# A three-layer graph network kernel: the normalised rows are split to fp16 before they are transposed, and the DMA queue transposes them

## The chip, the cores and the metric

The kernel runs on one core of one Trainium2 chip. The metric is the time of one launch on the device, in microseconds (us). The engines are PE (matrix products), ACT (activations and copies), DVE (element-wise work and statistics), POOL (element-wise work, SBUF only) and SP, which only issues DMAs. Each runs its own list of instructions in order, and they meet through semaphores.

## The reference

The input is 128 graphs of 128 nodes with 256 features, in float32, and an adjacency matrix for each. The rows are normalised and clipped at zero, then three layers of attention over neighbours and a feed-forward block of width 1024 follow, and the input is added at the end.

```python
h = jnp.maximum(_layernorm(x), 0.0)
for l in range(3):
    si, sj = x @ attn_w[l, :d], x @ attn_w[l, d:]
    scores = si[:, :, None] + sj[:, None, :] + attn_b[l]
    scores = where(scores >= 0, scores, 0.2 * scores); scores = where(mask, scores, -inf)
    agg = einsum('bij,bjd->bid', softmax(scores), x)
    h = layernorm(x + agg, g1[l], beta1[l])
    ff = gelu(h @ W1[l] + b1[l]) @ W2[l] + b2[l]
    x = layernorm(h + ff, g2[l], beta2[l])
```

## The kernel before

Four graphs (T = 4) are one group, and one layer of one group is an item: 32 groups by 3 layers make 96 items. The items go in rings of RING = 4 groups: four groups in layer 0, the same four in layer 1, then in layer 2. All five engines run the same list of slots (L119); a slot has 8 steps, c = 0 to 7, one for each block of 128 hidden features (L440, L540, L714). The program is written out in full; there are no loops on the chip.

Every float32 product is made of three fp16 products: hi by hi, lo by hi, hi by lo, where hi is the value rounded to fp16 and lo is the rest.

Slot s works on several items at once. In step c the feed-forward block of item s makes hidden block c: PE (L357, 6 matmuls), ACT a Gelu in place and a rounding to g_hi (L477), DVE the rest g_lo (L569). PE then uses block c - 3 for the second product (`feed`, L373, 12 matmuls). PE may be three hidden blocks ahead of g_lo (PF_RING), so the first hidden product of the next slot waits for g_lo of step 5.

Between these stands the attention of item s + 2: dot products of its rows with two vectors (`dot_products`, L606, DVE, step 1), their spread over columns by PE transposes (L398, step 4), scores, row maxima and `minus_max` (L625, L635, DVE, step 4), exponentials (L507, ACT, after step 5; they need another activation table, loaded before them and another one after), PE transposes of the probabilities (`transpose_probs`, L410, step 7). In step 0 of the next slot, where it is item s + 1, PE makes the sums over neighbours (`aggregate`, L416). DVE adds them to the rows and takes statistics (L649 and L660, at the end of its step 7, though PE's part stands in the next slot's step 0; L582 aggregates them in step 0), POOL makes the inverse deviation (L786), and ACT writes the normalised rows norm1 (`norm_attention`, L500, after step 2).

Norm1 of item s + 1 is then turned: PE transposes it in float32 in 8 pieces (`transpose_norm1`, L429, step 4) into the PSUM banks that the second product of item s + 1 will use; ACT rounds the result to hT_hi (`high_hT`, L530, step 4); DVE makes hT_lo from PSUM (`split_hT`, L669, step 5). hT_hi and hT_lo have two buffers each. The first hidden product of the next slot waits for hT_hi, its fifth matmul for hT_lo.

POOL goes through its slot in this order (L838): inverse deviation, `h_residual` (L793, two passes over 1024 elements, from norm1), `low_X` (L805, one pass, writes X_lo), then for item s - 1 the inverse deviation, `norm_feed` (L809) and `layer_output` (L818, four passes of 512). In layer 2 the output goes to y_out, and `skip_connection` (L831) adds the input.

Each slot whose item s + 4 is in layer 0 also loads, normalises and masks a new group (DVE steps 5 and 6, ACT step 7): 32 of the 96. SP issues the loads and the stores, in an order of its own (L330 to L351). The PSUM is full: three banks of hidden blocks, one for scores and probabilities, and four in two pairs.

Of the kernel before, what the change touches and what calls it, by code (L numbers as in the profile page):

```python
# [41 lines left out]
RING = 4  # L42
# [55 lines left out]

def is_item(r, s):
    return not isinstance(r, int) or 0 <= PER * r + s < ITEMS  # L100
# [29 lines left out]
def gnn_kernel(nc, x, adj, attn_w, attn_b, W1, b1, W2, b2, g1, beta1, g2, beta2, out):  # L130
    with ExitStack() as ctx:
# [12 lines left out]
        minus_half = sb("minus_half", [P, T])  # L144
        w1_f32 = sb("w1_f32", [P, KD, H])
# [21 lines left out]
        x_again = [sb(f"x_again{i}", [P, T, D]) for i in range(2)]  # L167
        y_out = [sb(f"y_out{i}", [P, T, D]) for i in range(2)]
# [19 lines left out]
        hT_hi = [sb(f"hT_hi{i}", [P, KD, TN], F16) for i in range(2)]  # L188
        hT_lo = [sb(f"hT_lo{i}", [P, KD, TN], F16) for i in range(2)]
# [23 lines left out]

        def nT_banks(s):
            return p_pair[s % 2][:].rearrange("p (k u) d -> p k (u d)", k=KD)
# [33 lines left out]
        nT_psum = sem("nT_psum")  # L249
# [25 lines left out]
        def _(sp):  # L275
            def weights(l):
                if l >= 1:
                    sp.wait_ge(w_lo_ready, 4 * l - 2)
                    sp.wait_ge(bias_psum, l)
                sp.dma_start(w1_f32[:], W1[l].rearrange("(k p) h -> p k h", p=P)).then_inc(w_dma[0], 16)  # L280
                if l >= 1:
                    sp.wait_ge(w_lo_ready, 4 * l)
                sp.dma_start(w2_f32[:], W2[l].rearrange("(c p) d -> p c d", p=P)).then_inc(w_dma[1], 16)

            def graphs(tensor, g):

                v = tensor.rearrange("(g t) n d -> n g t d", t=T)
                if isinstance(g, int):
                    return v[:, g]
                return v[:, bass.ds(g, 1)].rearrange("n g t d -> n (g t) d")  # L290

            def load_x(g, i):
                sp.dma_start(x_in[i][:], graphs(x, g)).then_inc(x_loaded[i], 16)

            def load_adj(g, i):
                sp.dma_start(adj_in[i][:], graphs(adj, g)).then_inc(adj_loaded[i], 16)

            def load_again(g, i):
                sp.dma_start(x_again[i][:], graphs(x, g)).then_inc(x_again_loaded[i], 16)

            def store(g, i):
                sp.dma_start(graphs(out, g), y_out[i][:]).then_inc(stored[i], 16)

            load_x(0, 0)
            load_adj(0, 0)
# [7 lines left out]
            load_x(1, 1)  # L313
            load_adj(1, 1)
            weights(0)
            for g in (2, 3, 4, 5):
                sp.wait_ge(x0_ready, 4 * (g - 1))
                load_x(g, g % 2)
                sp.wait_ge(mask_steps, 2 * (g - 1))
                load_adj(g, g % 2)  # L320
                if g == 2:
                    for dst, v in ((g1_rows, g1), (b2_rows, b2), (res_rows, beta1), (g2_rows, g2), (beta2_rows, beta2)):
                        sp.dma_start(dst[:].rearrange("p l d -> p (l d)"),
                                     flat(v).partition_broadcast(P)).then_inc(rows_dma, 16)
                if g in (3, 4):
                    weights(g - RING + 2)
            load_again(0, 0)
            load_again(1, 1)

            for r in range(LOOPS - 1):  # L330
                for q in range(RING):
                    i, g = q % 2, r * RING + q

# [8 lines left out]
            for g in range(RING * (LOOPS - 1), G):  # L342
# [7 lines left out]
                if g + 2 < G:  # L350
                    load_again(g + 2, g % 2)  # L351
# [421 lines left out]
        def _(pool):  # L773
# [64 lines left out]
            def slot(r, s):  # L838
# [6 lines left out]
                if is_item(r, s + 2):  # L845
                    low_X(r, s + 2)
# [32 lines left out]
```

## Time and profile before

| | before |
|---|---|
| median of 3 runs | 2461.77 us (2460.39 to 2462.76) |
| profiled execution, own time | 2464.22 us |
| its span | 2462.4 us |
| PE, DVE, ACT, POOL busy | 95%, 85%, 77%, 69% |
| granted TensorE clock, mean | 0.993 |

PE stands near its limit over the whole span, and DVE not far below. A share of busy time does not say what sets the length of a slot, so a slot has to be followed in the order of time. In the rows below, times are microseconds from the start of the span, and the first two numbers of a row are start and length. A row with "x4" holds four instructions that follow one another, and its length is that of all four. Instructions that overlap in an engine's pipe show lengths that are greater than the distance of their starts.

### The profile page before, as it was taken

How to read it: one execution, taken by the hardware profiler on the slowest of the kernel's cores; microseconds unless marked ns; L12 is line 12 of the kernel's file. 1: busy time of each engine (PE TensorE's matmuls, PEld its weight loads, DVE VectorE, ACT ScalarE, POOL GpSimd, SP SyncE). 2: the span in 40 equal slices, each digit the busy share in tenths (PEclk: the TensorE clock that was granted, in tenths of full speed). 3: DMA queues.
4: the chain of work that ended last, by engine and by line, in shares of the span. 5: the costliest groups of instructions: out<-in, count | busy, mean ns of one | idle time of the engine just before them, and what ended most of it. 6: DMA issues, size and time to landing. Idle time of an engine off the chain costs nothing.

```text
span 2462.4 us, 47718 instructions
## 1 busy us (share of the span) xinstructions
PE 2350.7 (95%) x16608; PEld 1648.4 (67%) x16608; DVE 2097.8 (85%) x6070; ACT 1890.0 (77%) x3402; POOL 1701.0 (69%) x1540
## 2 busy tenths in 40 slices
PE   3999999999999999999999999999999999999997
PEld 2766666676666666667666666666666666666765
DVE  6778998888988899888988889988898889988884
ACT  4767788877787878787787777877778777878783
POOL 3457677767776767766786667776678676777675
PEclk9999999999999999999999999999999999999998
DMA  5200012000210002100021001200012000110001
GB/s 170 73 1 1 1 44 78 1 1 1 74 48 1 1 14 61 48 1 1 14 78 31 1 1 31 73 18 2 1 44 61 18 2 1 44 52 1 1 1 52
DMA packets 77422, 70.84 MB, mean 29 GB/s; under 512 B 7040, under 2 KB 75648, under 8 KB 77184
## 3 DMA queue, kind: packets, MB, share of 16 engines
q1 hardware_dynamic: 77184, 67.79, 9.1%
q8 instruction: 134, 2.20, 0.4%
q14 instruction: 104, 0.85, 0.1%
HBM read 51.01 MB, written 16.78 MB: 28 GB/s over the span
## 4 chain that ended last, share of the span: by engine, by line
DVE 55%; PE 19%; ACT 13%; issue 10%; POOL 0%; DVEq 0%; POOLq 0%
DVE g_lo L573 11%; DVE bn L580 9%; PE p_pair L383 8%; DVE res L656 6%; DVE dots L614 6%; ACT probs L514 5%; PE p_hid L369 5%; ACT L514 5%; DVE res L681 5%; DVE scores L632 4%; DVE dots L617 4%; PE p_pair L425 3%; DVE row_top L638 3%; DVE minus_max L642 2%; PE p_att L413 2%
## 5 line engine op out<-in xcount | busy, mean ns | idle before, releaser
L383 PE MATMUL p_pair<-w_hi,g_hi 128*128 128x256 f16 x3072 | 839.1, 273 | 0.0
L383 PE MATMUL p_pair<-w_lo,g_hi 128*128 128x256 f16 x3072 | 838.8, 273 | 0.0
L383 PE MATMUL p_pair<-w_hi,g_lo 128*128 128x256 f16 x3072 | 838.8, 273 | 0.0
L481 ACT ACTIVATE p_hid<-p_hid,b_eff 128x512 f32<-128x512 f32 x768 | 504.5, 657 | 328.6 <-PE p_hid L369 327.4
L573 DVE TENSOR_TENSOR g_lo<-p_hid,g_hi 128x512 f16<-128x512 f32 x768 | 527.5, 687 | 239.4 <-ACT g_hi L486 232.9
L801 POOL TENSOR_TENSOR h_res<-norm,g_rows 128x1024 f32<-128x1024 f32 x96 | 227.7, 2372 | 395.8 <-DVE res L681 389.1
L486 ACT ACTIVATE g_hi<-p_hid 128x512 f16<-128x512 f32 x768 | 458.5, 597 | 24.3
L369 PE MATMUL p_hid<-hT_hi,w_hi 128*128 128x512 f16 x1536 | 458.7, 380 | 2.3 <-DVE g_lo L573 2.3
L369 PE MATMUL p_hid<-hT_hi,w_lo 128*128 128x512 f16 x1536 | 458.9, 380 | 0.0
L369 PE MATMUL p_hid<-hT_lo,w_hi 128*128 128x512 f16 x1536 | 458.8, 380 | 0.0
L789 POOL TENSOR_TENSOR rstd<-var_eps,minus_half 128x4 f32<-128x4 f32 x224 | 241.6, 1079 | 307.4 <-DVE minus_mean L588 302.1
L383 PEld LDWEIGHTS p_pair<-w_lo,g_hi 128*128 128x128 f16 x3072 | 301.2, 98 | 107.3 <-issue 0.8
L383 PEld LDWEIGHTS p_pair<-w_hi,g_hi 128*128 128x128 f16 x3072 | 301.2, 98 | 106.2 <-issue 1.0
L383 PEld LDWEIGHTS p_pair<-w_hi,g_lo 128*128 128x128 f16 x3072 | 301.2, 98 | 35.5
L491 ACT ACTIVATE norm<-res,shift,rstd 128x256 f32<-128x256 f32 x384 | 199.3, 589 | 102.0 <-POOL shift L791 102.0
L369 PEld LDWEIGHTS p_hid<-hT_lo,w_hi 128*128 128x128 f16 x1536 | 150.8, 98 | 182.6 <-issue 2.5
L369 PEld LDWEIGHTS p_hid<-hT_hi,w_lo 128*128 128x128 f16 x1536 | 150.7, 98 | 182.5 <-issue 2.2
L580 DVE BATCH_NORM_STATS2 bn<-res 128x6 f32<-128x256 f32 x768 | 268.9, 414 | 3.3
L803 POOL TENSOR_TENSOR h_res<-h_res,res_rows 128x1024 f32<-128x1024 f32 x96 | 226.9, 2363 | 7.5
L587 DVE TENSOR_SCALAR var_eps<-mv 128x4 f32<-128x4 f32 x224 | 213.4, 953 | 7.7
L815 POOL TENSOR_SCALAR norm<-res,rstd,shift 128x256 f32<-128x256 f32 x384 | 209.8, 561 | 10.0
L656 DVE SCALAR_TENSOR_TENSOR res<-p_pair,row_inv,X 128x256 f32<-128x256 f32 x384 | 159.0, 477 | 65.5 <-PE p_pair L425 65.5
(67 smaller groups left out, 3855.2 us busy)
## 6 DMA issues: line engine op xcount, KB each, us to landing
x_in<-in_x SPq DMA_DIRECT2D x32, 512.0 KB, 5.3
x_again<-in_x SPq DMA_DIRECT2D x32, 512.0 KB, 5.1
out<-y_out SPq DMA_DIRECT2D x32, 512.0 KB, 3.3
adj_in<-in_adj SPq DMA_DIRECT2D x32, 256.0 KB, 5.6
w_f<-in_L_gnn_W SPq DMA_DIRECT2D x6, 1024.0 KB, 5.6
attn_rows<-in_L_gnn_attn_w SPq DMA_DIRECT2D x1, 768.0 KB, 5.6
g_rows<-in_L_gnn_g SPq DMA_DIRECT2D x2, 384.0 KB, 8.3
b_rows<-in_L_gnn_b SPq DMA_DIRECT2D x1, 384.0 KB, 7.4
```

What stands on the lines that cost most here:

```text
L369: mm = pe.matmul(p_hid[in_ring(s, c, PF_RING)][:], w[l][:, k, cols], h[i][:, k, :], start=(n == 0), stop=(n == 3 * KD - 1))
L383: mm = pe.matmul(ff_banks(s)[:, t, :], g[i][:, nodes], w[l][:, c, :], start=(c == 0 and t % 2 == 0 and n == 0), stop=(c == C - 1 and n == ...
L481: act.activation(p_hid[k][:], p_hid[k][:], ACT.Gelu, bias=b1_eff[:, l, c:c + 1], scale=1.0 / WSCALE).then_inc(gelu_ready, 1)
L486: act.activation(g_hi[i][:], p_hid[k][:], ACT.Copy).then_inc(g_hi_ready, 1)
L514: act.activation(probs[:, t, :], leaky[:, t, :], ACT.Exp, bias=minus_max[:, t:t + 1], accum_out=row_sum[:, t:t + 1]).then_inc(probs_ready, 1)
L573: dve.tensor_tensor(g_lo[i][:], p_hid[k][:], g_hi[i][:], ALU.subtract).then_inc(g_lo_ready, 1)
L580: dve.bn_stats(bn[n][:, t, :], src[:, t, :]).then_inc(stat_steps[n], 1)
L587: dve.tensor_scalar(var_eps[n][:], mv[n][:, :, 1], EPS, None, ALU.add).then_inc(stat_steps[n], 1)
L656: dve.scalar_tensor_tensor(out=res1[:, t, :], in0=agg_banks(s)[:, t, :], scalar=row_inv[:, t:t + 1], in1=X[s % RING][:, t, :], op0=ALU.mul ...
L789: pool.tensor_tensor(rstd[n][s % 2][:], var_eps[n][:], minus_half[:], ALU.pow).then_inc(rstd_ready[n], 1)
L801: pool.tensor_tensor(h_res[i][:], norm1[:], rows(g1_rows, l, T), ALU.mult).then_inc(h_res_steps, 1)
L803: pool.tensor_tensor(h_res[i][:], h_res[i][:], rows(res_rows, l, T), ALU.add).then_inc(h_res_steps, 1)
```

## The change

- The 8 float32 transposes of norm1 on PE are gone. ACT rounds norm1 to h_hi in SBUF (`high_h`) in step 3, ahead of `high_X`, where `high_hT` stood in step 4. DVE makes h_lo = norm1 - h_hi, both inputs in SBUF (`low_h`), in step 4, ahead of the scores, where `split_hT` stood in step 5. SP issues two DMA transposes of 128x1024 fp16 for each item (`turn_h`); h_hi and h_lo have one buffer each.
- RING is 8. Eight groups go through a layer before the next layer begins, so rows of layers 1 and 2 are ready six slots before their attention.
- The dot products of items in layers 1 and 2 move from step 1 (item s + 2) to step 5 (item s + 3), where DVE waits for ACT. Those of layer 0 stay in step 1. POOL waits for the moved ones ahead of its inverse deviation for item s - 1.
- On DVE, two tensor_scalar instructions on 4 elements (`var_eps`, `minus_mean`) become tensor_tensor with constant tiles, and the scalar_tensor_tensor of `minus_max` becomes two tensor_tensor.
- The buffers y_out and x_again lie in w1_f32 and w2_f32, which are free once the weights are split. SP's order is written by slot, and skip_connection stands ahead of the inverse deviation.

```diff
-RING = 4
+RING = 8
@@ sync
+            def turn_h(r, s):
+                i = s % 2
+                if later(r, s, 2):
+                    sp.wait_ge(hid_psum, total(r, s - 2, C, C))
+                for h, hT, made, turned in ((h_hi, hT_hi, h_hi_ready, hT_hi_ready), (h_lo, hT_lo, h_lo_ready, hT_lo_ready)):
+                    sp.wait_ge(made, total(r, s, 1, 1))
+                    sp.dma_start_transpose(hT[i][:].rearrange("p t k n -> p (t k) n"),
+                                           h[:].rearrange("p t d -> p (t d)")).then_inc(turned, 16)
@@ tensor
-            def transpose_norm1(r, s):
-                if later(r, s, 2):
-                    pe.wait_ge(res2_ready, total(r, s - 2, 2, 2))
-                pe.wait_ge(norm1_ready, total(r, s, 4, 4))
-                for k in range(KD):
-                    for t in range(T):
-                        mm = pe.transpose(nT_banks(s)[:, k, t * N:(t + 1) * N],
-                                          norm1[:, t, k * P:(k + 1) * P], ident[:])
-                mm.then_inc(nT_psum, 1)
@@ scalar
-            def high_hT(r, s):
-
-                act.wait_ge(nT_psum, total(r, s, 1, 1))
-                if later(r, s, 2):
-                    act.wait_ge(hid_psum, total(r, s - 2, C, C))
-                act.activation(hT_hi[s % 2][:], nT_banks(s), ACT.Copy).then_inc(hT_hi_ready, 1)
+            def high_h(r, s):
+                act.wait_ge(norm1_ready, total(r, s, 4, 4))
+                if later(r, s):
+                    act.wait_ge(hT_hi_ready, total(r, s - 1, 16, 16))
+                act.activation(h_hi[:], norm1[:], ACT.Copy).then_inc(h_hi_ready, 1)
...
+                    if c == 3 and is_item(r, s + 1):
+                        high_h(r, s + 1)
                     if c == 3 and is_item(r, s + 2):
                         high_X(r, s + 2)
-                    if c == 4 and is_item(r, s + 1):
-                        high_hT(r, s + 1)
@@ vector
-                dve.tensor_scalar(var_eps[n][:], mv[n][:, :, 1], EPS, None, ALU.add).then_inc(stat_steps[n], 1)
+                dve.tensor_tensor(var_eps[n][:], mv[n][:, :, 1], eps_row[:], ALU.add).then_inc(stat_steps[n], 1)
...
-                dve.scalar_tensor_tensor(out=minus_max[:], in0=row_top[:], scalar=SLOPE, in1=row_top[:],
-                                         op0=ALU.mult, op1=ALU.min).then_inc(score_steps, 1)
+                dve.tensor_tensor(minus_max[:], row_top[:], slope_row[:], ALU.mult).then_inc(score_steps, 1)
+                dve.wait_ge(score_steps, total(r, s, 7, 6))
+                dve.tensor_tensor(minus_max[:], minus_max[:], row_top[:], ALU.min).then_inc(score_steps, 1)
...
+            def low_h(r, s):
+                dve.wait_ge(h_hi_ready, total(r, s, 1, 1))
+                if later(r, s):
+                    dve.wait_ge(hT_lo_ready, total(r, s - 1, 16, 16))
+                dve.tensor_tensor(h_lo[:], norm1[:], h_hi[:], ALU.subtract).then_inc(h_lo_ready, 1)
...
-                    if c == 1 and is_item(r, s + 2):
+                    if c == 1 and is_item(r, s + 2) and layer_of(s + 2) == 0:
...
+                    if c == 4 and is_item(r, s + 1):
+                        low_h(r, s + 1)
                     if c == 4 and is_item(r, s + 2):
                         add_scores(r, s + 2)
                         row_maxima(r, s + 2)
...
+                    if c == 5 and is_item(r, s + 3) and layer_of(s + 3) > 0:
+
+                        dot_products(r, s + 3, 0)
+                        dot_products(r, s + 3, 1)
@@ gpsimd
+                    if is_item(r, s + 3) and layer_of(s + 3) > 0:
+
+                        pool.wait_ge(dots_ready, total(r, s + 3, 8, 8))
                     inverse_deviation(s - 1, 2, total(r, s - 1, 10, 10), total(r, s - 1, 2, 1))
```

## Rows read from the trace of the kernel before

**Rows 1.** Busy time of each engine in one slot: us, then busy (x instructions)

```profile
1364.30:1388.60 24.30, 24.06 (x174) 16.91 (x172) 20.42 (x60) 18.94 (x35) 16.42 (x15) 1.00 0.01 1
```

**Rows 2.** Waits of the whole run: engine, line, releaser, us, times, longest

```profile
PEld p_att L413 <- ACT probs L514: 90.6, 94, 4.9
ACT leaky L509 <- DVE minus_max L642: 67.7, 93, 9.2
```

**Rows 3.** PE in order of time, one slot: start, length, instruction [idle before]

```profile
1356.61 0.66 PE L413 MATMUL p_att<-ident,probs 128*128 128x128 f32 x4 [0.24 <-ACT probs L514]
1358.41 0.59 PE L369 MATMUL p_hid<-hT_hi,w_hi 128*128 128x512 f16 x2
...
1372.75 1.04 PE L435 MATMUL p_pair<-ident,norm 128*128 128x128 f32 x8
1373.62 0.60 PE L407 MATMUL p_att<-ident,s_j 128*128 128x128 f32 x4
...
1380.96 0.66 PE L413 MATMUL p_att<-ident,probs 128*128 128x128 f32 x4 [0.24 <-ACT probs L514]
```

**Rows 4.** DVE in order of time, the same slot

```profile
1362.53 1.66 DVE L656 SCALAR_TENSOR_TENSOR res<-p_pair,row_inv,X 128x256 f32<-128x256 f32 x4 [0.97 <-PE p_pair L425]
...
1367.42 0.48 DVE L614 CUSTOM_DVE_ANT_0 dots<-X,attn_rows,attn_b_col 128x256 bf16<-128x256 f32 x1
...
1370.42 0.69 DVE L573 TENSOR_TENSOR g_lo<-p_hid,g_hi 128x512 f16<-128x512 f32 x1
...
1374.86 1.12 DVE L632 SCALAR_TENSOR_TENSOR scores<-p_att,s_i,mask 128x128 f32<-128x128 f32 x4
...
1376.73 0.56 DVE L642 SCALAR_TENSOR_TENSOR minus_max<-row_top 128x4 f32<-128x4 f32 x1
```

**Rows 5.** ACT in order of time, the same slot

```profile
1368.34 2.07 ACT L491 ACTIVATE norm<-res,shift,rstd 128x256 f32<-128x256 f32 x4 [0.62 <-POOL shift L791]
...
1371.47 1.05 ACT L528 ACTIVATE X_hi<-X 128x1024 f16<-128x1024 f32 x1
1372.42 0.65 ACT L481 ACTIVATE p_hid<-p_hid,b_eff 128x512 f32<-128x512 f32 x1
1373.11 0.60 ACT L486 ACTIVATE g_hi<-p_hid 128x512 f16<-128x512 f32 x1
```

**Rows 6.** POOL in order of time, the same slot

```profile
1372.48 2.36 POOL L801 TENSOR_TENSOR h_res<-norm,g_rows 128x1024 f32<-128x1024 f32 x1 [4.17 <-DVE res L681]
...
1377.22 2.13 POOL L807 TENSOR_TENSOR X_lo<-X,X_hi 128x1024 f16<-128x1024 f32 x1
```

**Rows 7.** POOL in order of time, in the first slots

```profile
49.26 2.12 POOL L807 TENSOR_TENSOR X_lo<-X,X_hi 128x1024 f16<-128x1024 f32 x1
```

**Rows 8.** DVE in order of time, in the first slots

```profile
27.87 0.16 DVE L642 SCALAR_TENSOR_TENSOR minus_max<-row_top 128x4 f32<-128x4 f32 x1
...
49.89 2.57 DVE L566 SCALAR_TENSOR_TENSOR w_lo<-w_f,w_hi 128x1024 f16<-128x1024 f32 x1
...
54.65 1.22 DVE L566 SCALAR_TENSOR_TENSOR w_lo<-w_f,w_hi 128x1024 f16<-128x1024 f32 x1
```

**Rows 9.** PE in order of time, around 165 us

```profile
165.16 0.66 PE L413 MATMUL p_att<-ident,probs 128*128 128x128 f32 x4 [4.25 <-ACT probs L514]
```

**Rows 10.** DVE in order of time, in the same slot as rows 9

```profile
172.76 1.66 DVE L656 SCALAR_TENSOR_TENSOR res<-p_pair,row_inv,X 128x256 f32<-128x256 f32 x4 [2.65 <-PE p_pair L425]
```

**Rows 11.** Busy time by stretch; the third number from the end is the clock

```profile
165.00:168.00 3.00, 2.84 (x17) 2.16 (x18) 0.26 (x1) 2.94 (x6) 2.92 (x4) 0.70 0.00 0
...
171.00:174.00 3.00, 3.00 (x24) 2.11 (x23) 1.24 (x4) 0.43 (x1) 0.00 (x0) 1.00 0.03 5
```

**Rows 12.** DVE in order of time: scores of two slots that load a group

```profile
1200.54 1.12 DVE L632 SCALAR_TENSOR_TENSOR scores<-p_att,s_i,mask 128x128 f32<-128x128 f32 x4
...
1226.14 1.12 DVE L632 SCALAR_TENSOR_TENSOR scores<-p_att,s_i,mask 128x128 f32<-128x128 f32 x4
```

**Rows 13.** DMA issues: xcount, KB each, median us from issue to landing

```profile
beta_rows<-in_L_gnn_beta SPq DMA_DIRECT2D x1, 384.0 KB, 8.8
```

More of the change, by code:

```diff
@@ L96, in x_total, with group_of @@
     return (4 * PER + RING) * r + v if isinstance(r, int) else r * (4 * PER + RING) + v
+def group_of(r, s):
+    return RING * (r + s // PER) + s % RING
 def is_item(r, s):
@@ L187, in gnn_kernel @@
         h_res = [sb(f"h_res{i}", [P, T, D]) for i in range(2)]
-        hT_hi = [sb(f"hT_hi{i}", [P, KD, TN], F16) for i in range(2)]
-        hT_lo = [sb(f"hT_lo{i}", [P, KD, TN], F16) for i in range(2)]
+        h_hi, h_lo = sb("h_hi", [P, T, D], F16), sb("h_lo", [P, T, D], F16)
+        hT_hi = [sb(f"hT_hi{i}", [P, T, KD, N], F16) for i in range(2)]
+        hT_lo = [sb(f"hT_lo{i}", [P, T, KD, N], F16) for i in range(2)]
         g_hi = [sb(f"g_hi{i}", [P, TN], F16) for i in range(GS_RING)]
@@ new lines, in slot @@
+            def slot(r, s):
+                if is_item(r, s + 2) and layer_of(s + 2) == 0 and group_of(r, s + 2) + 2 < G:
+                    sp.wait_ge(x0_ready, group_total(r, s + 2, 4, 4))
+                    load_x(group_of(r, s + 2) + 2)
+                if is_item(r, s + 3) and layer_of(s + 3) == 0 and group_of(r, s + 3) + 2 < G:
+                    sp.wait_ge(mask_steps, group_total(r, s + 3, 2, 2))
+                    load_adj(group_of(r, s + 3) + 2)
+                if (r, s) == (0, -2):
+                    for dst, v in ((g1_rows, g1), (b2_rows, b2), (res_rows, beta1), (g2_rows, g2), (beta2_rows, beta2)):
+                        sp.dma_start(dst[:].rearrange("p l d -> p (l d)"),
+                                     flat(v).partition_broadcast(P)).then_inc(rows_dma, 16)
+                if (r, s) in ((0, -1), (0, 1)):
+                    weights((s + 3) // 2, 0)
+                if is_item(r, s - 3) and layer_of(s - 3) == L - 1:
+                    store(r, s - 3)
+                if is_item(r, s + 1):
+                    turn_h(r, s + 1)
+                if (r, s) in ((0, -1), (0, 1)):
+                    weights((s + 3) // 2, 1)
+                if (r, s) == (0, 5):
+                    sp.wait_ge(w_lo_ready, 4 * L)
+                    load_again(0)
+                    load_again(1)
@@ L821, in layer_output @@
                 dst = y_out[q % 2] if l == L - 1 else X[q]
+                if l == L - 1 and not later(r, s, 2 * RING + 2):
+                    pool.wait_ge(w_lo_ready, 4 * L)
                 if l == L - 1 and later(r, s, 2 * RING + 2):
```

134 lines of the change are left out of this document (52 added, 82 removed).

## The prediction, made before the changed kernel was run

> **What bounds the kernel now.** I read four views in this order: the busy times of one slot, the waits of the whole run, then one slot in the order of time on PE, DVE, ACT and POOL, and last the first slots, where the order is disturbed. In the quiet slot PE works 24.06 of 24.30 us and no other engine over 20.42 [rows 1]. That looks like a kernel that PE alone bounds, and the change takes work off PE. The reader is to see in the waits that this is half of it: 94 times PE's probability transposes wait for the exponentials on ACT, and 93 times ACT waits, ahead of them, for `minus_max` on DVE [rows 2]. So each slot has a closed chain beside PE's own work, and I measure it. A slot lasts from one probability transpose to the next, 1380.96 - 1356.61 = 24.35 us [rows 3]. The chain in it: from the transpose PE needs 5.92 us (its four transposes, two hidden and two feed blocks, the sums over neighbours) until DVE begins the residual at 1362.53 [rows 3, 4]. DVE, with little idle time, ends `minus_max` at 1376.73 + 0.56 = 1377.29, 14.76 us later [rows 4]. ACT's leaky step, table load and exponentials bring the next transpose 3.67 us later, at 1380.96 [rows 3]. The sum is 5.92 + 14.76 + 3.67 = 24.35, the whole slot. The rule to work with: **if `minus_max` ends x us later after the residual begins, the slot is x us longer.** If it ends earlier, PE's own work is the floor.
>
> **PE.** The 8 transposes take 1373.62 - 1372.75 = 0.87 us of PE's time [rows 3]. Without them, and without the wait before the probability transposes (from row to row about 0.4 us), PE's floor is 24.35 - 0.87 - 0.4 = 23.1 us. They are not in the chain above, since DVE and ACT are later there anyway; this saving counts only if the chain falls under 23.1, so that `minus_max` ends by 1376.0. Reading hT in runs of 128 columns costs PE nothing in my sum; no row shows such reads beside whole ones, and I give it 0 to 0.1 us.
>
> **The dot products.** They take 1370.42 - 1367.42 = 3.00 us of DVE in the chain [rows 4], and leave it in the slots whose item s + 2 is in layer 1 or 2, 64 of 96. What is late next is ACT: norm1 begins at 1368.34, the next thing after it is hidden block 3, and before, X_hi began 3.13 us and hidden block 4 4.08 us after the start of norm1 [rows 5]. DVE cannot make g_lo 4 before ACT's g_hi 4.
>
> **The rounding of norm1.** `high_h` has the shape of X_hi, whose step on ACT is 1372.42 - 1371.47 = 0.95 us [rows 5], and stands ahead of it. Hidden block 4 so begins at 1373.37 and its g_hi 0.69 later, ending at 1374.66; DVE starts g_lo 4 at 1374.69, where it began 1374.25 before (0.61 ahead of the scores, [rows 4]). So the 3.00 us taken from DVE return nothing in the chain: ACT is 0.44 us later than DVE used to be. In the 32 slots that keep their dot products in step 1 DVE comes at 1374.25 and waits for the same g_hi. The copy that `high_hT` made after block 4 goes; it was beside the chain.
>
> **The rest of norm1.** `low_h` stands between g_lo 4 and the scores, so all of it is in the chain; `split_hT` was behind `minus_max`, outside. Its nearest row is L566, which also subtracts an fp16 tile from a float32 tile of 1024 elements, both in SBUF: 1.22 us, or 1.13 from start to start [rows 8]. It can start at 1374.69 + 0.60 = 1375.29. Here comes the costliest question. At 49.89 the same L566 took 2.57 us: POOL's X_lo pass had begun at 49.26, ended at 51.38, and L566 ended 1.08 us after that [rows 7, 8]. `minus_max`, again two inputs in SBUF, took 0.16 us with POOL idle and 0.56 in the quiet slot, ending at 1377.29 just after POOL's L803 gives way to X_lo at 1377.22 [rows 4, 6, 8]. I conclude that such a DVE instruction waits until the POOL pass in front of it ends. The Trainium skill, "SBUF — State Buffer", section "Who interferes with whom", says it as a rule: a DVE instruction with two SBUF inputs contends with a POOL instruction that reads SBUF, tensor_tensor included, and the first to start holds the port. By that rule the change of three tiny instructions to tensor_tensor buys nothing either, and the rows agree with it.
>
> So where does POOL stand at 1375.29? Its `h_residual` began at 1372.48 because it waited for DVE's residual, which now comes about 3 us earlier; norm1 then decides, at 1368.34 + 2.07 = 1370.41. Two passes and the gap take 1377.22 - 1372.48 = 4.74 us [rows 6], so X_lo begins near 1375.2 and holds until 1377.3, 2.13 us later. `low_h` comes under 0.1 us behind it. In the 32 slots with early dot products POOL still starts near 1372.5, and `low_h` waits for its second pass until 1377.2. Both give `low_h` the port at about 1377.3. I take this, the waiting value: `low_h` ends its step at 1378.5, scores and maxima take 1376.73 - 1374.86 = 1.87 as before [rows 4], and the two small instructions 0.35, since POOL is then idle. `minus_max` ends at 1380.7 in place of 1377.29: **3.4 us later**, a slot of 27.8 us. The bounds for `low_h`: 1.1 us with the port free, which gives 1378.7 and a slot of 25.8; 3.2 us with the wait.
>
> **PE's clock.** PE loses its cover: it has done all before the probability transposes at about 1380.96 - 0.4 - 0.87 = 1379.7 [rows 3] and starts them at 1380.7 + 3.67 = 1384.4. It idles 4.7 us in each slot. One slot of before shows what such a pause does: after 4.25 us [rows 9] the granted clock of the next stretch was 0.70, part of it at 1.2 GHz, and full (2.4 GHz) from 171 us on [rows 11]. The way from the transposes to the residual then took 172.76 - 165.16 = 7.60 us [rows 9, 10] where it takes 5.92, so 1.68 more. That stretch lies in the chain. I take it for every slot: 27.8 + 1.7 = 29.5 us. The bounds are 0 and 1.7.
>
> **DMA transposes.** They are new. h_hi is ready at 1368.34 + 3.13 + 1.05 = 1372.5, h_lo at 1378.5. The next slot's first hidden product starts at 1384.4 + 1.8, or somewhat later at the low clock, and wants hT_lo 0.9 us on: 14 us for hi, 8.6 for lo. No row shows a transpose. The dearest plain transfer landed after 8.8 us [rows 13], and nothing bounds it from below but zero. If each takes up to 8 us and they run one after the other, nothing waits; I take 0. Queued on SP behind them are loads and stores of the next slot, which have more than a slot to spare; SP's wait for h_lo holds them back some 8 us and nobody waits. The Trainium skill, "VectorE: DVE Perf Modes", section "The three transpose paths", gives 1.309 us for one 128x128 transpose on the DMA crossbar; if the 16 of an item came one after the other, that would be an estimated 21 us, and hT_lo would be late. No run here shows it yet.
>
> **The rest.** RING 8, y_out in the weights' buffers and SP's order have room: weights are split by slot 3, and the first y_out is written in slot 17. POOL waits for the dot products of step 5, which end some 6 us after `minus_max`; its later passes (1.3 + 2.2 + 5.3 us) still end before the next inverse deviation. The 3.0 us of dot products now fall into DVE's wait for the exponentials: cost 0; uncovered it would be 3.0. The 32 slots that load a group take 1226.14 - 1200.54 = 25.60 us [rows 12]; their extra 1.25 comes from POOL and DVE being late, which the longer slot covers, so they too come to 29.5.
>
> **The sum.** About 90 slots of the 96 are regular, 62 quiet and 28 loading. 62 x (29.5 - 24.35) = 319 and 28 x (29.5 - 25.6) = 109, together 428 us. On the profiled span of 2462.4 this is 2890; the time of that execution was 2464.22, 1.8 above its span, and the median of the runs is 2461.77, so I say **2890 us**.
>
> **The rivals.**
> (A) As forecast, but the clock does not fall: 62 x 3.4 + 28 x 3.0 = 295, so about 2757. For it: only one pause of this length stands in the regular part of the trace.
> (B) `low_h` comes just before X_lo, or is not held by POOL at all. The margin is under 0.1 us, and L566 is a scalar_tensor_tensor. Then two thirds of the slots are 1.4 us longer, and the others 1.4 to 3.4. The mean is +1.4 to +2.1, less in loading slots, and gives 2560 to 2625; with the clock falling after pauses of 2.7 us it is up to 2780. Its middle is 2640.
> (C) The DMA transposes are late. It decides from 8 us each: hi and lo at 8.8 us end at 1372.5 + 17.6 = 1390.1, some 1.3 us behind the need in a slot of 29.5. 90 x 1.3 = 117 gives about 3010, and each further us of both costs two more in each slot.
> (D) Faster: the chain falls to PE's floor. The mechanism is that g_lo 4 is not held by ACT and `low_h` is free, because fp16 operands let DVE and ACT go at twice the rates of the rows, and the 3.00 us of dots count. It decides where `minus_max` ends by 1377.29. With all of it PE's 23.1 us rule: 62 x 1.25 + 28 x 2.5 = 148, so 2315. Against it: X_hi and L566 already have these types.
> (E) The change does not do what it says, that is, nothing moves because the chain is not closed as I read it: within 0.2%.
>
> **How the numbers follow.** Forecast 0.44, A 0.12, B 0.27, C 0.08, D 0.05, E 0.02, and 0.02 for other slower ends. The likeliest gives 2890. The range takes in B's middle, the forecast and C's first step: 2590 to 3010; outside are D, E, the ends of B and C, together some 0.15 to 0.2. Faster 0.05, same 0.02, slower 0.93; a measurement of this kernel tells about 0.2% from no change.
>
> **What would show it.** Right: slots near 29.5 us; `low_h` rows of 3.1 us or so that end with POOL's X_lo or its second h_res pass; ACT's g_hi 4 ahead of DVE's g_lo 4 as releaser; pauses of 4 to 5 us before the probability transposes, with a granted clock near 0.9 or less over a slot. Wrong: `low_h` rows of 1.2 us (B), a clock of 1.0 in spite of the pauses (A), PE waiting at L369 for a DMA (C), PE without pauses (D).

## The result, and the profile after

The changed kernel takes **2975.23 us** (median of 4 runs, 2974.55 to 2976.94) where the kernel before takes 2461.77: a ratio of 1.2085, 95% interval 1.207 to 1.21. It is slower, as forecast, by 513 us where 428 were forecast; the time lies within the range of 2590 to 3010.

The span and the granted clock of the changed kernel, 0.896 in the mean:

```profile
core 0: 2973.3 us, clock 0.896
```

and its waits of the whole run, which answer to [rows 2]:

```profile
DVE g_lo L568 <- ACT g_hi L482: 516.8, 395, 5.1
...
ACT leaky L505 <- DVE minus_max L639: 472.7, 94, 8.6
...
PE p_att L421 <- ACT probs L510: 451.6, 94, 10.0
```

The last of them reads in the kernel before:

```profile
PE p_att L413 <- ACT probs L514: 44.4, 94, 4.5
```

ACT's wait for `minus_max` grew from 67.7 us to 472.7, PE's wait for the exponentials from 44.4 us to 451.6, which is 4.8 us a slot. The engines form the same chain as before, only later. The slot from 1634.42 on, one whose dot products stand in step 1, shows where. DVE, answering to [rows 4]:

```profile
1643.15 1.66 DVE L652 SCALAR_TENSOR_TENSOR res<-p_pair,row_inv,X 128x256 f32<-128x256 f32 x4 [2.51 <-PE p_pair L433]
...
1655.37 0.69 DVE L568 TENSOR_TENSOR g_lo<-p_hid,g_hi 128x512 f16<-128x512 f32 x1 [0.53 <-ACT g_hi L482]
1655.98 2.98 DVE L669 TENSOR_TENSOR h_lo<-norm,h_hi 128x1024 f16<-128x1024 f32 x1
...
1661.01 0.16 DVE L639 TENSOR_TENSOR minus_max<-minus_max,row_top 128x4 f32<-128x4 f32 x1
```

From the residual to the end of `minus_max` it is 1661.17 - 1643.15 = 18.02 us, where it was 14.76; `low_h` takes 2.98 us of it. POOL in the same slot, answering to [rows 6]:

```profile
1655.54 2.35 POOL L809 TENSOR_TENSOR h_res<-h_res,res_rows 128x1024 f32<-128x1024 f32 x1
1657.84 3.11 POOL L813 TENSOR_TENSOR X_lo<-X,X_hi 128x1024 f16<-128x1024 f32 x1
```

POOL in a slot whose dot products are in step 5:

```profile
1406.72 2.13 POOL L813 TENSOR_TENSOR X_lo<-X,X_hi 128x1024 f16<-128x1024 f32 x1
```

and DVE in that one:

```profile
1406.85 3.08 DVE L669 TENSOR_TENSOR h_lo<-norm,h_hi 128x1024 f16<-128x1024 f32 x1
```

The reader is to see the ends. In the first slot POOL's second h_res pass ends at 1657.89 and `low_h` 1.07 us later, at 1658.96; in the second X_lo began 0.13 us ahead of `low_h`, ended at 1408.85, and `low_h` 1.08 us later. In the first, X_lo in turn took 3.11 us instead of 2.13, because `low_h` was ahead of it. So it is in all 89 regular slots: in 63 `low_h` begins 0.10 to 0.13 us behind X_lo, in 26 it begins during the second h_res pass. PE, and its clock by stretch (busy times of PE, PEld, DVE, ACT, POOL, then the clock), answering to [rows 9, 11]:

```profile
1634.42 1.11 PE L421 MATMUL p_att<-ident,probs 128*128 128x128 f32 x4 [4.38 <-ACT probs L510]
...
1664.85 1.11 PE L421 MATMUL p_att<-ident,probs 128*128 128x128 f32 x4 [4.38 <-ACT probs L510]
```

```profile
1628.00:1631.00 3.00, 2.04 (x13) 1.00 (x11) 2.90 (x12) 0.22 (x1) 2.53 (x1) 1.00 0.45 85
1631.00:1634.00 3.00, 0.00 (x0) 0.00 (x0) 2.18 (x8) 2.97 (x9) 2.44 (x5) 0.90 0.02 3
1634.00:1637.00 3.00, 2.58 (x12) 2.06 (x13) 0.00 (x0) 2.94 (x6) 0.94 (x2) 0.50 0.00 0
1637.00:1640.00 3.00, 3.00 (x11) 1.36 (x9) 2.86 (x12) 2.97 (x6) 1.00 (x1) 0.50 0.03 5
1640.00:1643.00 3.00, 3.00 (x27) 2.54 (x26) 0.64 (x2) 1.79 (x4) 2.84 (x4) 0.97 0.40 109
```

After a pause of 4.4 us the clock stands at its lower level, 1.2 GHz (0.50), through two whole stretches, in which PE is busy from 1634.42 on. The transposes take 1.11 us, not 0.66, and the residual comes 1643.15 - 1634.42 = 8.73 us after them, not 5.92.

I took the three terms of the slot from 89 consecutive slots of each trace (means; what lies before the sixth of the 96 probability transposes and behind the last but one is the ends):

| | transposes to residual | residual to leaky step | leaky step to transposes | slot | ends |
|---|---|---|---|---|---|
| before | 6.02 | 15.13 | 3.64 | 24.79 | 256.2 us |
| after | 8.31 | 18.41 | 3.64 | 30.36 | 270.8 us |

89 x (30.36 - 24.79) = 496 us, and the ends 14.6: together the 511 us between the spans. Of the slot's 5.57 us, 3.28 are the later `minus_max` and 2.29 the longer way from the transposes to the residual, which I put down to the clock; the third experiment tests it.

### The profile page after: what moved, and what is told of

The parts are those of the page before. It is cut to its first block, busy times and chain, and to the rows that moved or that the text cites. A ratio compares the mean times of both kernels' runs of the same rounds, so it can differ in the third digit from the quotient of the medians.

```text
span 2973.3 us, 46572 instructions
## 1 busy us (share of the span) xinstructions
PE 2477.1 (83%) x15840; PEld 1673.4 (56%) x15840; DVE 2121.3 (71%) x6166; ACT 1896.1 (64%) x3402; POOL 1747.6 (59%) x1543
## 4 chain that ended last, share of the span: by engine, by line
DVE 31%; PE 29%; ACT 24%; issue 12%; POOL 4%; SPq 0%; DVEq 0%; DMA 0%; ACTq 0%; POOLq 0%
PE p_pair L391 13%; DVE h_lo L669 9%; PE p_hid L377 7%; ACT norm L487 6%; DVE res L652 5%; ACT probs L510 5%; PE p_pair L433 4%; ACT L510 4%; DVE bn L575 4%; PE p_att L421 4%; ACT p_hid L477 3%; DVE scores L627 3%; POOL rstd L795 3%; ACT X_hi L524 3%; DVE g_lo L568 3%
## 5 line engine op out<-in xcount | busy, mean ns | idle before, releaser
L391 PE MATMUL p_pair<-w_hi,g_hi 128*128 128x256 f16 x3072 | 891.0, 290 | 0.0
L391 PE MATMUL p_pair<-w_lo,g_hi 128*128 128x256 f16 x3072 | 890.3, 290 | 0.0
L391 PE MATMUL p_pair<-w_hi,g_lo 128*128 128x256 f16 x3072 | 889.5, 290 | 0.0
L377 PE MATMUL p_hid<-hT_hi,w_hi 128*128 128x512 f16 x1536 | 492.8, 405 | 1.9 <-DVE g_lo L568 1.9
L377 PE MATMUL p_hid<-hT_hi,w_lo 128*128 128x512 f16 x1536 | 486.4, 400 | 0.0
L421 PE MATMUL p_att<-ident,probs 128*128 128x128 f32 x384 | 106.0, 431 | 451.6 <-ACT probs L510 451.6
L391 PEld LDWEIGHTS p_pair<-w_hi,g_hi 128*128 128x128 f16 x3072 | 322.4, 105 | 127.0 <-issue 14.2
L505 ACT ACTIVATE leaky<-scores 128x512 f32<-128x512 f32 x96 | 60.4, 629 | 472.7 <-DVE minus_max L639 472.7
L421 PEld LDWEIGHTS p_att<-ident,probs 128*128 128x128 f32 x384 | 68.2, 215 | 498.2 <-ACT probs L510 497.8
L669 DVE TENSOR_TENSOR h_lo<-norm,h_hi 128x1024 f16<-128x1024 f32 x96 | 290.6, 3027 | 0.6 <-ACT h_hi L530 0.6
```

Source lines behind the costliest of these rows:

```text
L377: mm = pe.matmul(p_hid[in_ring(s, c, PF_RING)][:], w[l][:, k, cols], h[i][:, :, k, :], start=(n == 0), stop=(n == 3 * KD - 1))
L391: mm = pe.matmul(ff_banks(s)[:, t, :], g[i][:, nodes], w[l][:, c, :], start=(c == 0 and t % 2 == 0 and n == 0), stop=(c == C - 1 and n == ...
L421: mm = pe.transpose(p_att[:, t, :], probs[:, t, :], ident[:])
L669: dve.tensor_tensor(h_lo[:], norm1[:], h_hi[:], ALU.subtract).then_inc(h_lo_ready, 1)
```

## The experiments

Four kinds of questions: is it `low_h` behind POOL, is it the clock, what did the other parts do, and does a shorter chain make a kernel that beats both.

**low_h out of the chain.**

```diff
-                    if c == 4 and is_item(r, s + 1):
-                        low_h(r, s + 1)
...
+                    if c == 5 and is_item(r, s + 1):
+                        low_h(r, s + 1)
```

> The changed kernel with low_h moved from step 4 to step 5 of DVE, behind minus_max, where split_hT stood. Chain theory: low_h (3.0 us with its wait) leaves the chain from the residual to minus_max, which falls from 18.04 us to 15 to 17 us (minus_max can still wait for a POOL pass), PE's pause before the probability transposes shrinks from 4.3 us to 1 to 3 us and the clock falls less or not at all: 2480 to 2620 us. Rival, the DMA transposes or the new order of the rings carry the loss: low_h's place hardly matters and the time stays over 2850 us. Should the DMA transpose of h_lo (3.1 us) come too late for the next slot, PE waits at its fifth hidden matmul, and the time is over the range of the chain theory.

Measured: 2664.27 us (one run), clock 0.947. DVE, first in a slot with early dot products, then in a quiet one:

```profile
1377.12 2.13 DVE L637 TENSOR_TENSOR minus_max<-row_top,slope_row 128x4 f32<-128x4 f32 x1
1379.29 2.26 DVE L639 TENSOR_TENSOR minus_max<-minus_max,row_top 128x4 f32<-128x4 f32 x1
...
1578.40 0.16 DVE L637 TENSOR_TENSOR minus_max<-row_top,slope_row 128x4 f32<-128x4 f32 x1
1578.60 0.16 DVE L639 TENSOR_TENSOR minus_max<-minus_max,row_top 128x4 f32<-128x4 f32 x1
...
1579.84 1.22 DVE L669 TENSOR_TENSOR h_lo<-norm,h_hi 128x1024 f16<-128x1024 f32 x1
```

Of the 511 us 311 are gone, so `low_h`'s place is the main cause (the way from the residual to the leaky step is 16.45 us in the mean, not 18.41, and with shorter pauses the way to the residual is 6.87, not 8.31). With POOL idle `low_h` takes 1.22 us. Half of the slots come to 24.9 us. The other half, around the early dot products and the skip connection, stay at 27 to 30.6; the first two lines show the dearest case, a slot with both. Two instructions on four numbers a partition take 2.13 and 2.26 us there, one behind each of two POOL passes (X_lo, then the skip connection). I had not counted on that, and so the time is 44 us over the expected range.

**POOL's passes out of the way.** h_res's two passes and X_lo work on 4 of 256 columns of one of the four graphs; the rest of these tiles stays zero, so part of the residual and of the sums is left out.

```diff
...
-                pool.tensor_tensor(X_lo[:], X[s % RING][:], X_hi[:], ALU.subtract).then_inc(X_lo_ready, 1)
+                pool.tensor_tensor(X_lo[:, 0:1, 0:4], X[s % RING][:, 0:1, 0:4], X_hi[:, 0:1, 0:4], ALU.subtract).then_inc(X_lo_ready, 1)
```

> The changed kernel with POOL's three passes of 1024 elements (both of h_residual and low_X) cut to 4 elements, so that most of the residual and of X_lo is left out. Everything else, with every semaphore, stays. Port theory: low_h meets no POOL pass and takes 1.2 us in place of 3.03, so the chain from the residual to minus_max is 18.04 - 1.8 = 16.2 us, the slot at the full clock 25.8 us; PE still pauses 2.7 us, with the clock between full and what it was: 2540 to 2780 us. Rival: low_h takes 3 us because of its own operands (both in SBUF, mixed types) and not because of POOL: its row stays at 3.0 us and the time over 2900 us.

Measured: 2727.07 us (one run), clock 0.931.

```profile
1520.08 1.22 DVE L669 TENSOR_TENSOR h_lo<-norm,h_hi 128x1024 f16<-128x1024 f32 x1
```

`low_h` stands in its old place, works on tiles of the same shapes and types, and takes 1.22 us. So its 1.8 further microseconds are the wait for POOL and nothing of its own. 248 us go with them: 1.99 us of each slot behind the residual, and 0.66 ahead of it, since PE now pauses for 2.5 to 3.1 us in nearly all slots. The clock still falls after every one of these pauses.

**The pause filled.** PE makes 40 matmuls on weights ahead of each probability transpose, into a bank that is written over later.

```diff
+                        if is_item(r, s):
+                            fill(r, s)
                         transpose_probs(r, s + 2)
```

> The changed kernel with 40 more matmuls of 256 columns (about 4.3 us at the full clock) in each slot ahead of the probability transposes, into PSUM banks that are free there; their results are used by nobody, and nothing is left out. Clock theory: the pause is filled, the granted clock rises from 0.896 to over 0.97, the way from the transposes to the residual falls from 7.3 to 8.9 us to 5.9, and the kernel gets faster although it does more: 90 slots of 27.6 to 29.7 us, 2700 to 2790 us. Rival: the longer way has another cause than the pause, and 40 more matmuls cost up to their own time: 2975 us or more.

Measured: 2800.03 us (one run).

```profile
core 0: 2798.2 us, clock 0.984
```

The kernel does more work and is 175 us faster. The way from the transposes to the residual falls from 8.31 to 6.24 us in the mean (5.92 in most slots); 89 x 2.07 = 184 us. `low_h` still waits, and the chain behind the residual is no shorter (18.57). This is the clock's share alone. The time is 10 us over the expected range because of the slots around the skip connection and the early dot products (up to 32.6 us): there PE mostly still pauses for 2.1 to 3.4 us behind the 40 matmuls, and in 12 of them the clock still falls.

**Less work for PE in the kernel before.** Two of the three products of the second feed block are left out, 8 matmuls in each slot that start 0.11 us apart, together 0.87 us of PE's work, as much as the transposes that the change removes. Part of the output is missing.

```diff
-                    for n, (g, w) in enumerate(((g_hi, w2_hi), (g_hi, w2_lo), (g_lo, w2_hi))):
+                    for n, (g, w) in enumerate(products[:1] if c == 1 else products):
```

> The kernel before with 8 of the 12 matmuls of the second product's block 1 left out (hi by lo and lo by hi), which are 8 x 0.109 = 0.87 us of PE in step 4, beside norm1's transposes and as long as they. Their part of the output is missing. Chain theory: PE's time ahead of the scores is not in the chain, so nothing or little is gained: 2430 to 2462 us, ratio 0.987 to 1.0 (the 28 loading slots may give back their waits). Rival, PE alone bounds the kernel: 90 x 0.87 = 78 us are gained, 2384 us, ratio 0.968.

Measured: 2458.58 us, ratio 0.9987 (0.9977 to 0.9996). A quiet slot stays at 24.36 us, and PE's busy time in it falls from 24.06 us to 23.46. PE's work at this place does not set the slot, though PE was busy for 99% of it.

**The small instructions as tensor_tensor, in the kernel before.**

```diff
-                dve.tensor_scalar(var_eps[n][:], mv[n][:, :, 1], EPS, None, ALU.add).then_inc(stat_steps[n], 1)
+                dve.tensor_tensor(var_eps[n][:], mv[n][:, :, 1], eps_row[:], ALU.add).then_inc(stat_steps[n], 1)
...
```

> The kernel before, with one small part of the change alone: var_eps and minus_mean are made by tensor_tensor with a constant row in place of tensor_scalar. My reading (a DVE instruction with two SBUF inputs waits for the POOL pass in front of it, whichever of the two forms it has) expects the same time, a ratio of 0.998 to 1.002, with the var_eps rows, 0.95 us in the mean in the kernel before, at 0.8 to 1.1 us. The rival, that tensor_tensor escapes POOL where tensor_scalar does not, expects var_eps rows of 0.1 to 0.2 us and a ratio of 0.99 to 1.0.

Measured: 2463.33 us, ratio 1.0006 (0.9997 to 1.0016).

```profile
L588 DVE TENSOR_TENSOR var_eps<-mv,eps_row 128x4 f32<-128x4 f32 x224 | 212.2, 947 | 7.7
```

947 ns in the mean, against 953 of the tensor_scalar. The form makes no difference, though one form reads one tile in SBUF and the other two: in the kernel before 133 of the 224 begin beside a POOL instruction, in this one 134, and in both they end 0.01 to 0.03 us behind it. In the changed kernel the rows are 0.17 us in the mean (x224); 219 of them begin when POOL is idle.

**The dot products back in step 1, in the changed kernel.**

```diff
-                    if c == 1 and is_item(r, s + 2) and layer_of(s + 2) == 0:
+                    if c == 1 and is_item(r, s + 2):
```

> The changed kernel with one part undone: all dot products stand in step 1 again, and POOL doesn't wait for them any more. My step says that taking their 3.00 us out of the chain returned nothing, since hidden block 4 on ACT and then POOL hold low_h anyway: the slots of layers 1 and 2 then look like those of layer 0 in the changed kernel (low_h 2.98 us, ending with POOL's second h_res pass), and the time stays within 15 us of 2975. The rival, that the moved dot products did return their 3 us in 64 slots and only other costs hid it, expects 3100 or more.

Measured: 2990.22 us (one run), at the edge of what was expected. Residual to leaky step is 18.05 to 18.07 us in the 62 slots without a skip connection, no more than in the changed kernel. What is longer are the slots with one: there are now 8 in 24 that have the dot products in step 1 too, not 4, and in each residual to leaky step is 20.16 us.

**The skip connection back behind norm_feed.**

```diff
-                if is_item(r, s - 2) and layer_of(s - 2) == L - 1:
-                    skip_connection(r, s - 2)
                 if is_item(r, s - 1):
...
                     norm_feed(r, s - 1)
+                if is_item(r, s - 2) and layer_of(s - 2) == L - 1:
+                    skip_connection(r, s - 2)
```

> The changed kernel with one part undone: POOL's skip_connection stands behind norm_feed again, not between low_X and norm_feed. In the trace of the changed kernel 4 slots of 24 have both the skip_connection and the early dot products; they last 31.2 to 32.6 us, and the second small instruction of minus_max takes 2.27 us there, ending with POOL's pass. If the new place costs what I read there (some 2.1 us in the chain of each of the 4 slots, and 0.3 us in the 4 other slots with a skip_connection), the whole is 96 / 24 x (4 x 2.1 + 4 x 0.3) = 38 us faster than 2975, near 2937, range 2915 to 2950. The rival, that those slots are long for the clock's or the early dot products' sake, expects 2965 to 2980.

Measured: 2954.15 us, ratio to the kernel before 1.1999 (1.1979 to 1.2019), so 21 us less. DVE of the changed kernel, then POOL in the same slot of it:

```profile
1504.92 2.27 DVE L639 TENSOR_TENSOR minus_max<-minus_max,row_top 128x4 f32<-128x4 f32 x1
```

```profile
1504.83 2.33 POOL L844 TENSOR_TENSOR w_f<-w_f 128x1024 f32<-128x1024 f32 x1
```

and DVE of this version, in a slot with both as well:

```profile
1496.98 0.16 DVE L639 TENSOR_TENSOR minus_max<-minus_max,row_top 128x4 f32<-128x4 f32 x1
```

An instruction of 0.16 us takes 2.27 when the skip connection (w_f is the tile that y_out shares) begins 0.09 us ahead of it. The mechanism is as I read it. The size is about half of the 38 us that I expected, and the time 4 us over the range: one slot of 24 still lasts 32.0 us.

**A shorter chain in the kernel before.** `minus_max` waits for POOL. The reduction ahead of it does not: 93 of its 96 rows begin during a POOL pass, and all take 0.69 us. The maximum of the leaky scores needs a reduction alone.

```diff
-                dve.tensor_reduce(row_top[:], scores[:], AX.X, ALU.max, negate=True).then_inc(score_steps, 1)
...
+                dve.wait_ge(leaky_ready, total(r, s, 1, 1))
...
-                dve.scalar_tensor_tensor(out=minus_max[:], in0=row_top[:], scalar=SLOPE, in1=row_top[:],
-                                         op0=ALU.mult, op1=ALU.min).then_inc(score_steps, 1)
+                dve.tensor_reduce(minus_max[:], leaky[:], AX.X, ALU.max, negate=True).then_inc(score_steps, 1)
```

> The kernel before, with the chain alone shortened: ACT applies the leaky step to the scores first, and DVE takes the negated row maximum from its output, straight into minus_max, while ACT loads the table of the exponentials. The reduction of 0.6 us and the small instruction that waits for POOL leave the way from the residual to the next probability transposes. If both PE's own work and this chain set the slot, the chain falls by some 1.3 us under PE's own 24.0 us, and a quiet slot goes from 24.35 to about 24.0: 62 x 0.35 = 22 us, and up to 1.2 us in each of the 28 slots that load a group, 33 us: ratio 0.977 to 0.993. If PE alone set the slot: 0.998 to 1.002.

Measured: 2470.49 us, ratio 1.0037 (1.0024 to 1.005): 0.4% slower, outside both ranges. ACT, one slot:

```profile
1451.42 0.62 ACT L509 ACTIVATE leaky<-scores 128x512 f32<-128x512 f32 x1
1452.86 1.28 ACT L515 ACT_TABLE_LOAD   x1 [0.82 <-DVE minus_max L641]
1454.16 0.40 ACT L515 ACTIVATE probs<-leaky,minus_max 128x128 f32<-128x128 f32 x1
```

The table load belongs to the first exponential and comes behind its wait. So it doesn't run beside the maximum, and 0.8 us are added where 0.6 were won in a quiet slot. One line ahead of the wait mends it (against the kernel of the run above):

```diff
+                act.activation(warm[:], leaky[:, 0, 0:1], ACT.Exp).then_inc(warm_steps, 1)
                 act.wait_ge(score_steps, total(r, s, 5, 5))
```

> The kernel before with the maximum taken from the leaky scores, as in the run before, and one more line: a one-column exponential ahead of ACT's wait for minus_max. In the run before, the table load of the exponentials stood behind that wait (77 us of idle time ahead of 94 table loads), so that the way from the leaky step to the probability transposes grew from 3.64 to 4.44 us and ate the 0.6 us won ahead of it. If the table load is what lost the gain, this way comes back to 3.7 to 3.9 us, a quiet slot is 24.0 us (5.92 + 14.21 + 3.85, or PE's own work), and the slots that load a group some 0.6 us shorter than 25.6: 62 x 0.35 + 28 x 0.6 = 38 us, 2424, ratio 0.980 to 0.992. If ACT waits for the maximum in any case, 1.00 to 1.005 as before.

Measured: **2417.78 us**, ratio 0.9815 (0.9799 to 0.9831). This beats both kernels.

```profile
1445.18 0.62 ACT L511 ACTIVATE leaky<-scores 128x512 f32<-128x512 f32 x1
1445.82 1.28 ACT L517 ACT_TABLE_LOAD   x1
1447.12 0.20 ACT L517 ACTIVATE warm<-leaky 128x1 f32<-128x1 f32 x1
1447.22 0.39 ACT L520 ACTIVATE probs<-leaky,minus_max 128x128 f32<-128x128 f32 x1
```

A quiet slot is 5.86 + 14.21 + 3.82 = 23.9 us. Now PE works nearly all the time (stretch, then PE's busy time), so by an estimate from this row a shorter chain alone could win at most 1.3% more:

```profile
1000.00:2000.00 1000.00, 986.53 (x7081) 698.62 (x7079) 844.99 (x2542) 802.29 (x1490) 722.89 (x654) 1.00 0.08 23
```

**The same on the changed kernel**, with `low_h` in step 5, `high_h` in step 4, the skip connection behind norm_feed, and the maximum of the leaky scores; first without and then with the early table load.

> The changed kernel with its dot products in step 5 and its DMA transposes kept, and with what lengthened its chain taken out of it: low_h stands behind the scores in step 5, high_h in step 4 behind hidden block 4, skip_connection behind norm_feed as before, and the maximum is taken from the leaky scores. By the chain, residual to minus_max falls under 14.8 us, no pause opens before the probability transposes, the clock stays at 1.00, and PE's own work of 23.1 to 24.0 us a slot rules: 90 x -0.4 to -1.3 against the kernel before, 2340 to 2430 us, ratio 0.95 to 0.99. The rival, that the DMA transposes come too late for PE when low_h stands in step 5 (it ends some 18 us after the residual, and PE wants hT_lo some 26 us after it), expects 2480 or more, with PE's waits at the hT_lo products.

> The changed kernel with low_h in step 5, high_h in step 4 behind block 4, skip_connection behind norm_feed and the maximum of the leaky scores, and now the one-column exponential ahead of ACT's wait for minus_max. Its quiet slots were 24.36 = 5.92 + 14.00 + 4.44 us; with the table load early 0.6 us less, 23.8, which is still above PE's own 23.1: 96 x 0.6 = 58 us less than 2500, near 2442, ratio 0.985 to 0.998. If the slots with late hT_lo or a fallen clock grow by what the chain gives back, 2470 to 2500.

Measured: 2499.62 us, ratio 1.0155 (1.014 to 1.017), and 2494.50, ratio 1.0126 (1.0111 to 1.0141). Both miss the ranges of the chain and fall into those of their rivals, late `hT_lo`. Waits of the second one:

```profile
PEld p_hid L379 <- DMA hT_lo<-h_lo: 112.1, 88, 2.7
```

The first has such a wait in 30 slots (46.5 us), the second in 88. In a slot of 24 us `low_h` in step 5 is too late for the transpose behind it; what the chain gives back, PE waits for `hT_lo`. The slots around the skip connection still last 26.5 and 29.6 us, and those with early dot products 25.1 to 26.1. In these the way from the transposes to the residual is 7.8 to 7.9 us, in the quiet ones 6.3. DVE and PE around the start of one of them, at 1271.31, and the clock:

```profile
1269.24 1.69 DVE L588 TENSOR_TENSOR var_eps<-mv,eps_row 128x4 f32<-128x4 f32 x1
...
1271.52 1.21 DVE L671 TENSOR_TENSOR h_lo<-norm,h_hi 128x1024 f16<-128x1024 f32 x1
```

```profile
1275.89 0.60 PE L379 MATMUL p_hid<-hT_lo,w_hi 128*128 128x512 f16 x2 [1.76 <-DMA hT_lo<-h_lo]
```

```profile
1271.00:1274.00 3.00, 2.69 (x20) 1.96 (x20) 3.00 (x6) 2.94 (x6) 2.74 (x5) 1.00 0.01 2
```

The clock stays full. `var_eps`, 0.16 us alone, waits for POOL's X_lo, `low_h` comes behind it, and PE waits 1.76 us for `hT_lo`. In the quiet slots `var_eps` is not held, and `low_h` begins 1.3 us ahead of the probability transposes and not 0.2 us behind them; these 1.5 us are the difference. So the 0.87 us that the DMA transposes free on PE were not won here. It is argued, and no run shows it, that only an earlier `low_h` could win them, and that one stands in the chain.

**var_eps and minus_mean on POOL**, in the version of 2418 us:

```diff
-                dve.tensor_scalar(var_eps[n][:], mv[n][:, :, 1], EPS, None, ALU.add).then_inc(stat_steps[n], 1)
...
+                pool.tensor_scalar(var_eps[n][:], mv[n][:, :, 1], EPS, None, ALU.add).then_inc(rstd_ready[n], 1)
...
```

> The kernel before with the maximum of the leaky scores and the early table load (2418 us), and one more step drawn from the waits on POOL's passes: var_eps and minus_mean are made by POOL itself, ahead of its pow, so that DVE doesn't stand behind POOL for them. In the trace of that version each slot that loads a group has three var_eps rows of 1.06 to 1.32 us on a DVE without any idle time, and lasts 24.8 or 25.7 us; the quiet ones, where PE works without pause, 23.9. If DVE's order bounds the loading slots, up to 3 us of it go there, and they come to 24.2 to 24.9: 28 x 0.4 to 0.9 = 11 to 25 us less, 2393 to 2407, ratio to the kernel before 0.972 to 0.978. If PE or POOL's longer way to norm1 (two more small passes of some 0.2 us) takes its place, 2415 to 2430, ratio 0.980 to 0.987.

Measured: 2434.98 us, ratio 0.9891 (0.9874 to 0.9907): a loss of 17 us, beyond even the rival's range. A slot that loads a group:

```profile
1521.43 0.53 POOL L789 TENSOR_SCALAR var_eps<-mv 128x4 f32<-128x4 f32 x1
1522.04 0.26 POOL L790 TENSOR_SCALAR minus_mean<-mv 128x4 f32<-128x4 f32 x1
1522.38 1.14 POOL L792 TENSOR_TENSOR rstd<-var_eps,minus_half 128x4 f32<-128x4 f32 x1
```

These slots grew from 24.8 and 25.7 us to 25.4 and 26.2. POOL, not DVE, is late there: with 0.8 us more ahead of each pow, norm1 comes later (ACT's waits for POOL's shift are 188 us, not 115).

## Why the prediction was right, and where its sizes were off

**The closed chain**: right. `minus_max` came 3.28 us later after the residual, and the slots grew by that and by the clock's share. Leaving out PE work equal to that of the transposes moved the kernel before by 0.1%, and with the shorter chain and the early table load its quiet slot fell from 24.36 to 23.9 us.

**The dot products and g_lo 4**: right. DVE waits for ACT's g_hi 4 (0.53 us in the slot shown), and `low_h` begins 12.8 us behind the residual in all 89 slots, with the dot products in the chain or out of it; forecast were 1375.29 - 1362.53 = 12.76. Taking the 3.00 us back into the chain in all slots left residual to leaky step at 18.06 us.

**low_h waits for POOL**: right, and the rival (B) fell. The rows are 2.98 and 3.08 us, the step 3.0 to 3.1 instead of 3.2. The whole from residual to `minus_max` was 18.02 instead of 14.76 + 3.4 = 18.16. Which pass holds it was right too, X_lo or the second h_res pass, though it hung on the 0.1 us by which X_lo begins first. The Trainium skill, "SBUF — State Buffer", section "Who interferes with whom", is borne out by the trace down to instructions on 4 elements (0.16 us against 2.27). As the prediction quotes it, it speaks of two SBUF inputs; `var_eps` as a tensor_scalar has one and waits as well (1.77 us behind X_lo).

**The clock** is the term that was mis-sized most. It falls, so (A) fell, and the filled pause gives its price. But I took 1.68 us, the one pause of before, as upper bound of a term that measured 2.29 in the mean and up to 2.9 (8.84 - 5.92) in single slots. In the kernel before the clock was at 1.2 GHz for about half as long. The stretch between those of [rows 11] reads

```profile
168.00:171.00 3.00, 3.00 (x16) 1.67 (x15) 1.80 (x4) 2.18 (x5) 2.75 (x3) 0.73 0.00 0
```

so that two stretches stood at 0.70 and 0.73, where after the pause of the slot shown two stood at 0.50. In the changed kernel the way to the residual mostly goes 7.2, 8.1, 8.5, 8.8, 8.9 us from slot to slot and then begins again; no run shows what sets this order. 89 x (8.31 - 7.60) = 63 us of the 83 that are missing between the spans.

**The skip connection** is a term that I left out. Its new place stood under "The rest" at nothing, with no look at what DVE does beside it. It cost 21 us, although part of that is hidden in the sum by the 18.02 that came in under 18.16; the net is 89 x (22.05 - 21.9) = 13 us. The ends bring another 15, where I had counted six slots at zero. 63 + 13 + 15 = 91; counting 90 slots where the table has 89, and 24.74 us for a slot of before where its mean was 24.79, takes back 8 to 9, which leaves the 83.

**The range** held by luck. Its upper end, 3010, stood there only for the late DMA transposes of (C), and they were not late. The forecast itself took `low_h` and the clock at their upper bounds, so it left no room above 2890 for what then came. In (A) the loading slots should have been 27.8 - 25.6 = 2.2 us longer, not 3.0: 62 x 3.4 + 28 x 2.2 = 272 us and not 295. The forecast does not use that sum.

**The DMA transposes cost nothing**: right. SP in the slot shown:

```profile
1653.22 1.24 SPq L317 DMA_TRANSPOSE hT_hi<-h_hi  x1
1658.99 1.23 SPq L317 DMA_TRANSPOSE hT_lo<-h_lo  x1
```

and the median from issue to landing:

```profile
hT_hi<-h_hi SPq DMA_TRANSPOSE x96, 3.0
hT_lo<-h_lo SPq DMA_TRANSPOSE x96, 3.1
```

`hT_lo` has landed at 1662.1, and PE first takes it at 1670.02; no wait for it stands in the trace, so (C) fell. The wait came up as soon as the slot was 24 us long and `low_h` late. The 21 us that I estimated from the Trainium skill, "VectorE: DVE Perf Modes", section "The three transpose paths", with the blocks one after the other, are not what the trace shows: 8 blocks land in 3.0 us.

**The order of the three small instructions** bought nothing by their form, as the fifth experiment shows. (D) and (E) fell with the result.

What is left open: which pauses make the clock fall. It stayed full where each quiet slot had a pause of 1.4 to 1.6 us, and fell where each had one of 2.5. After single pauses of 2.1 to 3.2 us in the other versions it did now the one, now the other. No run varied the pause alone. It is open, too, whether the DMA transposes can win anything once `low_h` no longer waits and comes early.

## What to carry over

When work is moved ahead of a critical instruction, look up not only its length but which shared thing it holds or waits for at that moment on the other engine, and do it for every moved step, the small ones too. An engine that is 99% busy may still not be what sets the time; and a pause that opens on TensorE has a second price, the clock behind it, which a single row doesn't bound from above. A range should be as wide as each term may be wrong, and not be held up by a rival that has nothing to do with it. A wait placed ahead of an ACT function of another table also delays the table load.

## What the runs showed of the hardware

- After a pause of 4.4 us TensorE stood at 1.2 GHz for two stretches of 3 us in the slot shown, and the clock fell in all 89 regular slots; 40 matmuls that compute nothing of use made the kernel 175 us faster by covering the pause.
- Pauses of 1.4 to 1.6 us in each quiet slot (the version with `low_h` in step 5) left the slots at 24.9 us and the way to the residual at 5.92: no fall of the clock there. Pauses of 2.5 us (short POOL passes) made that way 7.4 to 7.6 us.
- A DVE instruction of 4 elements a partition can wait as long for a POOL pass as one of 1024 does: 0.16 us alone, 2.26 behind the pass. It ends 0.02 us behind the pass, one of 1024 elements 1.08. POOL waits in turn: X_lo 3.11 instead of 2.13 us.
- A tensor_reduce from SBUF on DVE took 0.69 us in all 96 slots, though 93 began during a POOL pass (kernel before).
- A DMA transpose of 128x1024 fp16, within SBUF, lands after 3.0 us and keeps SP's queue for 1.23.
- The table load of ACT, 1.28 us, was not started while its instruction waited for a semaphore: it began 0.82 us late behind the wait for `minus_max`, and at once with an instruction of the same table ahead of that wait.
